# Writing out the 128 attention blocks and moving four small DMAs from ScalarE's queue to the loads' queue

## What is computed

```python
q = short_conv(x @ Wq, conv_q); k = short_conv(x @ Wk, conv_k); v = short_conv(x @ Wv, conv_v)   # 4 taps, silu
beta = 2 * sigmoid(x @ Wb);  g = -exp(A_log) * softplus(x @ Wa + dt_bias)
q = l2norm(q) * d ** -0.5;   k = l2norm(k)
def step(S, inp):
    qt, kt, vt, bt, gt = inp
    S = S * exp(gt)
    for i in range(3):
        S = S + bt[i] * outer(kt[i], vt[i] - kt[i] @ S)
    return S, qt @ S
...
o = o * rsqrt(mean(o * o) + 1e-5) * rms_weight * silu(x @ Wg)
x = layernorm(x + o @ Wo)
x = layernorm(x + experts(x))        # 8 experts, the two best of each token
```

## Time and profile before

| | us |
|---|---|
| timed runs: median (lowest, highest) of 3 | 4982.57 (4980.44, 4993.09) |
| span of the profiled execution | 4978.8 |
| PE busy | 4230.5 (85%) |
| PEld busy | 3759.0 (75%) |
| DVE busy | 3658.3 (73%) |
| ACT busy | 3285.0 (66%) |
| POOL busy | 1648.1 (33%) |

### The profile page before, as it was taken

How to read it: one execution, slowest core, us unless ns; L and a number is a source line. 1 busy time by engine, 2 the same in 40 slices (tenths; PEclk the granted TensorE clock), 3 DMA queues, 4 the chain that set the end, 5 groups by cost and what they waited for, 6 DMA issues and landing times. The chain is left out here.

```text
span 4978.8 us, 148669 instructions
## 1 busy us (share of the span) xinstructions
PE 4230.5 (85%) x47876; PEld 3759.0 (75%) x47876; DVE 3658.3 (73%) x10194; ACT 3285.0 (66%) x9028; POOL 1648.1 (33%) x1615
## 2 busy tenths in 40 slices
PE   2889988989898888898888898889889867599992
PEld 1788878888887777788788787888878745488882
DVE  6888888888888778788888788888888722344446
ACT  3777777777777677777777777777777611255552
POOL 3434333334433333343334343333434202200004
PEclk6999999999999999999999999999999877699996
DMA  6232223222223333222222222322222133366664
GB/s 234 69 95 73 66 77 86 79 70 77 77 71 70 76 77 70 70 77 79 82 75 77 77 67 77 92 76 67 75 77 75 43 88 108 123 236 227 230 236 140
DMA packets 363269, 490.64 MB, mean 99 GB/s; under 512 B 94080, under 2 KB 308096, under 8 KB 343680
## 3 DMA queue, kind: packets, MB, share of 16 engines
q1 hardware_dynamic: 304784, 437.06, 29.8%
q10 hardware_dynamic: 51568, 27.04, 1.9%
q0 software_dynamic: 6144, 16.79, 1.1%
HBM read 352.02 MB, written 107.75 MB: 92 GB/s over the span
## 5 line engine op out<-in xcount | busy, mean ns | idle before, releaser
L1134 DVE SCALAR_TENSOR_TENSOR conv_acc<-bank,c_cur,conv_acc 128x256 f32<-128x256 f32 x2688 | 1265.9, 477 | 274.3 <-ACT conv_acc L944 261.2
L692 PE MATMUL bank<-x_cur,w_cur 128*128 128x259 f16 (+1 forms) x6144 | 913.2, 288 | 29.4 <-DVE v_rows L1122 26.3
L1329 POOL TENSOR_TENSOR squares<-kq_t 128x768 f32<-128x768 f32 x128 | 187.7, 1467 | 1909.4 <-ACT kq_t L955 1909.4
L1195 DVE CAST_PREDICATED xs_lev<-mask,bank 128x256 f16<-128x256 uint16 x1536 | 662.2, 431 | 198.1 <-PE bank L756 174.4
L1002 ACT ACTIVATE invt<-bank 128x256 f16<-128x256 f32 x1280 | 509.7, 398 | 400.3 <-issue 374.5
L993 ACT ACTIVATE inv<-bank 128x256 f16<-128x256 f32 x1536 | 607.0, 395 | 167.8 <-PE bank L768 158.1
L692 PEld LDWEIGHTS bank<-x_cur,w_cur 128*128 128x128 f16 (+1 forms) x6144 | 577.7, 102 | 124.7 <-DVE v_rows L1122 27.2
L780 PE MATMUL bank<-invt,xs_lev 128*128 128x64 f16 x5120 | 379.9, 199 | 309.4 <-ACT invt L1002 305.2
L780 PEld LDWEIGHTS bank<-invt,xs_lev 128*128 128x128 f16 x5120 | 293.2, 101 | 341.5 <-ACT invt L1002 254.2
L944 ACT ACTIVATE conv_acc<-bank,c_cur 128x256 f32<-128x256 f32 x896 | 425.3, 475 | 156.5 <-PE bank L692 149.4
L824 PE MATMUL bank<-w_sol,k_rows 128*128 128x128 f32 x2048 | 474.6, 315 | 4.5 <-ACT w_sol L1012 4.1
(11 more groups left out here) (241 smaller groups left out, 10672.6 us busy)
## 6 DMA issues: line engine op xcount, KB each, us to landing
w_cur<-w_parts_scratch SPq DMA_DIRECT2D x128, 1024.0 KB, 7.1
ew<-e_parts_scratch SPq DMA_DIRECT2D x117, 896.0 KB, 6.2
x_cur<-x_parts_scratch SPq DMA_DIRECT2D x128, 259.0 KB, 7.0
x_slots<-no_rows SPq DMA_DIRECT2D x128, 256.0 KB, 7.1
e_parts_scratch<-e_pair SPq DMA_DIRECT2D x96, 224.0 KB, 6.0
o_rows<-w_sol ACTq DMA_DIRECT2D x512, 32.0 KB, 4.6
y_scratch<-y_buf SPq DMA_DIRECT2D x128, 128.0 KB, 6.3
y_in<-y_scratch SPq DMA_DIRECT2D x32, 512.0 KB, 4.1
```

Source lines behind the costliest of these rows:

```text
L692: last = mm(bank[i % 2][:, 0:PW], w_cur[k.i % 2][:, wp, kt, c * P:(c + 1) * P].bitcast(BF16 if wp else F16), x_cur[k.i % 2][:, xp, kt, 0:P ...
L1134: v.scalar_tensor_tensor(acc, bank[at % 2][:, i:i + TB], c_cur[k.i % 2][:, c, i:i + 1], acc, ALU.mult, ALU.add).then_inc(tap_step.sem if i ...
L1195: v.copy_predicated(half(xs_lev[g][l - 1][:], l, 0), half(mask4[:, l], l, 0).bitcast(U16), packed(halves(LEVX), l)).then_inc(x_kept.sem, 1)
```

## The change

All 128 blocks are written out on every engine, so every wait is on a constant, the `sem_inc` behind waits are gone, and `turn`, `blocks` and `Count.upto` know only whole numbers. Since addresses are constants too, the copies `c_cur`, `g_cur` and `t_cur` are dropped, and `conv_sb`, `g_parts` and `tables` are read in place. The four DMAs of `move_outputs` leave ACT's body; SP issues them in its turn n for block n-3, behind the loads for block n+1 and ahead of the clearing of `x_slots`.

```diff
-            def run_bodies(eng, body):
-                for i in range(UNROLL):
-                    body(*blocks(i, None, UNROLL))
-                with eng.Fori(1, NIT // UNROLL) as m:
-                    for i in range(UNROLL):
-                        body(*blocks(i, m, UNROLL))
-                for i in range(NIT, NIT + STAGES - 1):
-                    body(*blocks(i, None, UNROLL))
+            def run_bodies(body):
+                for i in range(NIT + STAGES - 1):
+                    body(*blocks(i))
...
                         sp.dma_start(w_cur[res][:].rearrange("p a b c -> p (a b c)"), w_dram[h]).then_inc(loaded[res], 16)
-                        sp.dma_start(c_cur[res][:], conv_sb[:, h]).then_inc(loaded[res], 16)
-                        sp.dma_start(g_cur[res][:], g_parts[:].rearrange("p n a -> p (n a)")[:, bass.ds((head * NTB + tb) * UN, UN)])\
-                            .then_inc(loaded[res], 16)
...
                     def load_next(tb, head):
                         n = B * H * tb + head
                         done(sp, projected, 7, n - 1)
-                        sp.sem_inc(sp_waited, 1)
                         done(sp, tapped, 6, n - 1)
-                        sp.sem_inc(sp_waited, 1)
-                        at_least(sp, g_made, n)
-                        sp.sem_inc(sp_waited, 1)
...
+                    def move_outputs(n):
+
+                        done(sp, sol_kept, 7, n)
+                        at_least(sp, scaled, n - 1)
+                        for c in range(4):
+                            sp.dma_start(o_rows[n % 2][c * CH:(c + 1) * CH], w_sol[n % 2][96:128, c::4, :]).then_inc(moved[n % 2], 16)
...
+                    for n in range(NIT):
+                        tb, head = n // (B * H), n % (B * H)
+                        if n + 1 < NIT:
                             load_next(tb, head)
+                        if n >= 3:
+                            move_outputs(n - 3)
+                        outputs(tb, head)
+                        pieces(tb, head)
...
-                    @at_stage
-                    def move_outputs(k):
-
-                        done(act, sol_kept, 7, k.n)
-                        at_least(act, scaled, k.n - 1)
-                        act.sem_inc(act_waited, 1)
-                        for c in range(4):
-                            act.dma_start(o_rows[k.i % 2][c * CH:(c + 1) * CH], w_sol[k.i % 2][96:128, c::4, :]).then_inc(moved[k.i % 2], 16)
...
                         silu(1, k0)
                         keep_t(4, 0, k1)
-                        move_outputs(k3)
                         keep_tt(4, 0, k1)
...
-                        dve.wait_ge(tabled[k.i % 4], 16 * (k.turn(4) + 1))
-                        v.tensor_tensor(c_n[k.i % 2][:], r2[k.i % 2][:], t_cur[k.i % 8][:, 0, :], ALU.mult)
+                        v.tensor_tensor(c_n[k.i % 2][:], r2[k.i % 2][:], tables[:, k.place, 0, :], ALU.mult)
...
                         done(dve, x_made, (l, g), k.n)
-                        dve.sem_inc(x_waited, 1)
```

More of the change, by code:

```diff
@@ L530, in build, with __init__, blocks @@
             class Block:
[L533 to L536, removed]
+                def __init__(self, n):
+                    self.n = self.i = n
+                    self.runs = 0 <= n < NIT
+                    self.h, self.place = n % H, n % (B * H) * NTB + n // (B * H)
                 def turn(self, ring):
-                    return self.i // ring if self.m is None else self.size // ring * self.m + self.i // ring
-            def blocks(i, m, size):
-                return [Block(i, m, s, size) for s in range(STAGES)]
+                    return self.n // ring
+            def blocks(i):
+                return [Block(i - s) for s in range(STAGES)]
             def at_stage(f):
@@ L681, in project @@
                         if i == 0:
-                            pe.wait_ge(loaded[k.i % 2], 64 * (k.turn(2) + 1))
+                            pe.wait_ge(loaded[k.i % 2], 32 * (k.turn(2) + 1))
                         if i >= 2:
@@ L943, in first_tap @@
                             done(act, silu_done, CHANNELS[5 + i], k.n - 1)
-                        a(conv_acc[(k.n + i) % 2][:], bank[i % 2][:, 0:TB], ACT.Copy, scale=c_cur[k.i % 2][:, c, 0:1])\
+                        a(conv_acc[(k.n + i) % 2][:], bank[i % 2][:, 0:TB], ACT.Copy, scale=conv_sb[:, k.h, c, 0:1])\
                             .then_inc(tap0.sem, 1)
@@ L1208, in right_side @@
                         done(dve, ks_made, c, k.n)
-                        v.scalar_tensor_tensor(rhs[k.i % 2][:], chain(k), t_cur[k.i % 8][:, 2, c:c + 1],
+                        v.scalar_tensor_tensor(rhs[k.i % 2][:], chain(k), tables[:, k.place, 2, c:c + 1],
                                                v_rows[k.i % R_ROWS][:, c], ALU.mult, ALU.add).then_inc(rhs_made.sem, 1)
@@ L1215, in new_state @@
                         s = state[:, k.i % (B * H)]
-                        v.scalar_tensor_tensor(s, s, t_cur[k.i % 8][:, 3, c:c + 1], chain(k), ALU.mult, ALU.add)\
+                        v.scalar_tensor_tensor(s, s, tables[:, k.place, 3, c:c + 1], chain(k), ALU.mult, ALU.add)\
                             .then_inc(stated.sem, 1)
@@ L1309, in g_rows @@
                     def g_rows(k):
-                        pool.wait_ge(loaded[k.i % 2], 64 * (k.turn(2) + 1))
                         done(pool, tt_made, "decays", k.n - 1)
-                        tt(g_upto[:], g_cur[k.i % 2][0:96, :, None].broadcast_to([96, UN, CH]),
+                        tt(g_upto[:], g_parts[0:96, k.place, :, None].broadcast_to([96, UN, CH]),
                            uptob[0:96, None, 0:CH].broadcast_to([96, UN, CH]), ALU.mult).then_inc(g_made, 1)
@@ L1381, in body @@
                         scale_outputs(k3)
-                    for head in range(B * H):
-                        body(0, head, *blocks(head, None, B * H))
-                    with pool.Fori(1, NTB) as tb:
-                        for head in range(B * H):
-                            body(tb, head, *blocks(head, tb, B * H))
-                    for i in range(NIT, NIT + STAGES - 1):
-                        body(None, i, *blocks(i, None, B * H))
+                    for i in range(NIT + STAGES - 1):
+                        body(*((i // (B * H), i % (B * H)) if i < NIT else (None, i)), *blocks(i))
         attention_scope.close()
```

76 lines of the change are left out of this document (20 added, 56 removed).

## The result

| | before | after |
|---|---|---|
| timed runs: median (lowest to highest) of 4 | 4981.5 (4950.02 to 4993.09) | 5058.49 (5002.33 to 5084.36) |
| span of the profiled execution | 4978.8 | 5082.6 |
| PE busy | 4230.5 | 4351.0 |
| DVE busy | 3658.3 | 3625.8 |

The change makes the kernel slower: the ratio is 1.0127, 95% interval 1.0073 to 1.0180. The forecast was 4957, faster; the time lies inside the range, on the wrong side of no change, and above the forecast's own 4905 to 5035: only the part of the range that belongs to rival (a) holds it.

What follows compares the result with a forecast made beforehand. PE, the fullest engine, was taken as held up by ACT issuing the moves and awaiting their landing. 4978.8 - 102 (landing) - 14 (jumps) + 90 (clock) gave 4953 on the span, 4957 timed; range 4810 to 5090.

Steps and rivals of the forecast that it cites:

- (a): Slower rival, at the squares (L1028): moves land no earlier, all 128 blocks pay for half clock; 5089 us timed, chance 0.25.
- The issues leave ACT: ACT in front of invt: 2.75 us of issuing a block go, so ACT comes to the squares earlier.
- The landing: Last move, before ACT's squares: lands 0.4 us earlier in 96 blocks, 2.0 us in 32; 102 us gained.
- Written-out blocks: At the loop's two backward jumps: idle time of about 7 us each goes, 14 us in all.
- What the new wait on SP holds up: SP behind the moves: clearing, stores and expert pieces come 1.8 us later; nobody in the loop waits for them.
- The clock: PE behind the squares: half clock moves there, costing 1.3 us in 96 blocks, 124 us; net 90 us lost.
- (b): Rival, TensorE's clock in the loop: one hole costs no more half clock than two; about 4844 us timed, chance 0.20.
- (c): Rival, ACT and PE waits: moves land early enough that ACT's time comes back whole; about 4605 us, chance 0.05.

Runs made afterwards that it cites:

- e1: The changed kernel with the four moves issued by ACT again, in their old place, blocks still written out: 4939.47 us, ratio 0.9939 to the kernel before.
- e7: The kernel before, loops and table copies kept, with SP issuing the moves ahead of its four loads: 4493.55 us, ratio 0.9002.
- e2: The changed kernel with two SP steps swapped, so the moves go ahead of the next block's loads: 4426.06 us, ratio 0.8892 to the kernel before.
- e9: The kernel before, loops and table copies kept, with SP issuing the moves behind its four loads: 5135.62 us, ratio 1.0323.
- e4: The changed kernel with 24 extra unread matmuls a block on PE in front of residual(0): 4888.80 us, ratio 0.9803 to the kernel before.
- e6: The changed kernel with 12 extra unread matmuls a block on PE in front of residual(0): 4892.33 us, ratio 0.9790 to the kernel before.
- e5: Against e1, moves still on ACT, SP's next loads wait until the moves have landed: 4665.85 us, ratio 0.9336 to the kernel before.
- e8: The changed kernel loading only the first half of w_cur from the third block on: 4531.15 us, ratio 0.9062 to the kernel before.
- e3: Against e1, moves still on ACT, SP's next loads wait until the moves may start: 5384.90 us, ratio 1.0824 to the kernel before.

## Why the prediction was wrong

**The issues leave ACT: right.** No idle "issue" in front of `invt` is left, and the idle time at the squares grew to 365.5 us, as announced ("over 250, most of the freed 374.5").

**The landing: right.** W+11.4 and W+9.4 were forecast. The last move lands at W+11.3 to 11.6 in five of the six usual groups (13.2 in the group that is late before too) and W+9.5 in groups 1 and 7. The gain from W to the squares is 96 x 0.46 + 32 x 1.98 = 107 us; the sum had 102.

**Written-out blocks: right in sign, too small.** 14 us were taken, and e1 shows about 30, or more: 1.2% and 1.9% with the moves on SP (e7 to e2, e9 to after). The jumps' 7 us are gone, but an idle time of that size is not. PE stands 23 times for over 1.2 us in the loop with nothing that the profile shows, 80 us in all and mostly in front of the squares, where it takes the place of the hole. The longest:

```profile
1839.74 0.38 PE L657 MATMUL bank<-x_cur,w_cur 128*128 128x259 f16 x1 [6.43 <-issue]
```

Before had 5 of them, e1 8 and e2 7, but e9, with its loops, has 20, so it is not the written-out code as such. The DMA records of the traces show what PE stands for: its instructions. Here a transfer of 16 KB of the instruction queue runs from 1837.29 to 1838.38, while `w_cur` is landing, and PE goes on 1.37 us behind its end. The same fits all 23 holes (1.2 to 1.6 us behind the end of such a transfer) and all 137 of the eleven traces (1.2 to 1.9), among them those at the two backward jumps of before; of moments taken at random only 5 to 7% lie 1.1 to 1.7 us behind one. The 23 holes end between W+8 and W+13.5, so the fetches seem to be held up by the loads, which no run tried; why there are 20 or more with the moves behind the loads (after, e4, e6, e9), 4 to 9 in e1, e2, e5, e7 and e8 and none in e3 is open as well.

**What the new wait on SP holds up: right.** Nobody in the loop waits for the clearing, the stores or the pieces.

**The clock: the step that failed.** The prediction took the price of half clock at 0.43 us for one, and that was right: 98 blocks of after with half clock behind the squares take 20.34 us for that stretch with 7.5 us at half clock, 25 without take 17.13 (means): 3.21 / 7.5, again 0.43. It also had the place right. The mis-sized term is the amount: "If the 3.0 us at half clock stay but move behind them". They did not stay: a usual block has 7.4 us at half clock behind the squares, and the loop 785 us instead of 345. At 0.43 the 7.4 us are 3.2 us a block where the sum had 1.3. (0.6 us of half clock stood there before, and the stretch at full clock became 0.5 us shorter, 17.1 where the 87 such blocks of before took 17.6, so less is seen.) In the measured balance the stretch from the squares to W costs 96 x 2.28 more and 32 x 0.30 less, 209 us, where the sum had 90 less the 14 of the jumps. With 4978.8 - 107 + 209 = 5081 the sum meets the span.

I had conserved a quantity that nothing conserves. TensorE fell to half clock about as often as before, but stayed there twice as long: 86 spells of 4.0 us on average in the loop of before, 98 of 8.0 in after. The length of the hole does not explain it alone, its place counts. Of 34 holes of 2.8 to 3.5 us in front of the squares in before, 28 were followed by half clock, for 4.0 us on average; of 33 such holes at the squares in after all were, for 7.8 us. Why it lasts longer there no run shows.

Block 28, which the prediction laid out, hid this, for with its two holes of 1.74 and 1.58 us and full clock throughout it was not typical: 79 of 123 blocks of before had over 1 us at half clock in front of the squares, behind a hole of 2.7 us (median), and then mostly no hole at the squares. Blocks 39 and 88 of before show both places, first PE's hole, then the clock behind it (columns as in the earlier trace rows):

```profile
1349.13 0.38 PE L780 MATMUL bank<-invt,xs_lev 128*128 128x64 f16 x4 [3.00 <-ACT invt L1002]
...
2852.17 0.29 PE L792 MATMUL bank<-inv,n_high 128*128 128x128 f16 x1 [2.74 <-ACT invt L1002]
```

```profile
1349.20:1352.50 3.30, 3.30 (x33) 2.84 (x34) 1.50 (x3) 1.85 (x7) 0.00 (x0) 0.50 0.65 211
2851.10:2861.20 10.10, 9.03 (x55) 8.69 (x56) 5.04 (x16) 5.32 (x17) 5.06 (x4) 0.50 0.01 3
```

In block 39 the clock is full again 0.7 us ahead of the squares (1353.34); in block 88 it is half for 10 us behind them. Blocks 15 and 88 were the only two of before with over 2.3 us of hole at the squares, and the evidence against the sum: in block 15 the hole of 2.86 us was followed by 6.8 us at half clock, twice the mean that I spread over all blocks. Taken as the price of every usual block, 6.8 x 0.43 x 96 = 281 less the 34.5 already paid gives 4863 + 246, or 5109 on the span: too high, but of the right sign.

**The rivals.** (a) came nearest in time, 5085 on the span, but by luck, for a false reason: it let the moves land no earlier, and they did. Its criterion was sound, that the change loses where the landing gains less than the clock costs: usual blocks gained 0.46 us there and paid 2.28. (b) fell in after; e4, whose clock is nearly full, comes to 4889 where (b) had 4844. (c) is what e2 does. It needed the moves ahead of the loads, not behind, and its 4605 was still too high by 180 us. No run splits these up; the half clock goes as well (14 us of it are left in the loop).

## What to carry to other kernels

Work that is taken off a busy engine is worth as much as the next wait allows. Look for the one that ends last there, and put the small transfer that it waits for ahead of the large one: two lines in the queue's order separate 5058 us from 4426. Before a hole of TensorE is moved or lengthened, read in the trace what clock followed the long holes that already stand in the new place, and charge every block that price, not the mean over the loop. And before one block stands for all, compare it with the mean of the loop, the clock too.

## What the runs showed of the hardware

- **A queue of their own does not keep small DMAs clear of a large one.** On ACT's queue (e1) the last move lands at W+12.2 on average, on SP's behind `w_cur` (after) at W+11.2, on ACT's with the first issue ahead of `w_cur` (e3) at W+11.4, and with half of the bytes (e8) at W+9.0. The Trainium skill, "DMA: Bandwidth & Descriptors", section Queues, rings and completion order, says that both queues share the 16 engines and that a completion count waits for every earlier write of its engine, of other queues too. By that rule the landing is `w_cur`'s whichever queue the moves use; these traces agree.
- **Two engines that issue at once slow each other.** ACT's last three issues took 4.99 us in block 20 of e3 beside SP's (4.95 in the median block), and 2.79 in block 20 of e5 with SP waiting (1.86 in the median). The Trainium skill, "Perfetto Trace Analysis", section DMA Instruction — HWDGE (DVE, Sync), has the descriptor generator locked for one sequencer at a time, with the wait for the lock inside the reported duration; the trace agrees.
- **More work on TensorE can take less time.** In after, 12 or 24 idle matmuls a block made the kernel 3% faster, by raising the mean granted clock of the loop from 0.90 to 0.96 and 0.98. TensorE fell to half clock behind holes of about 3 us, mostly (28 of 34 in front of the squares in before, 33 of 33 at the squares in after), and mostly stayed at full clock behind holes of 1.2 to 1.8 us (201 of 218 in the loops of before, after, e1, e4, e5 and e6); block 43 of after, with 2.79 us and full clock, shows that the hole alone does not decide.
- **TensorE can stand for its instructions.** In the attention loops of the eleven traces every one of the 137 stops of over 1.2 us that no semaphore explains ends 1.2 to 1.9 us behind a 16 KB transfer of the instruction queue. In after they are 23, 80 us, the longest 6.43 us.
